# A state-space scan on one Trainium2 core: where ScalarE's softplus and layer-norm passes stand among the scan's own instructions

## What is computed

```python
def _L2_attn_ref(x, in_proj_w, conv_w, conv_b, x_proj_w, dt_proj_w, dt_proj_b, A_log, out_proj_w):
    # x_in, z = in_proj(x);  x_conv = silu(causal conv of x_in)
    B_ssm, C_ssm = ssm_params[..., :N], ssm_params[..., N:2 * N]       # N = 16 states
    dt = jax.nn.softplus(ssm_params[..., -1:] * dt_proj_w[None, None, :, 0] + dt_proj_b)
    dA = jnp.exp(dt[..., None] * A[None, None])
    dBx = dt[..., None] * B_ssm[:, :, None, :] * x_conv[..., None]
    # for every t:  h = dA_t * h + dBx_t;  y_t = sum over n of h[n] * C_t[n]
    y = y * jax.nn.silu(z)
    return jnp.einsum('btd,ed->bte', y, out_proj_w)

x = x + _L2_attn_ref(_layernorm(x, axis=-1), ...)
x = x + _L2_ffn_ref(_layernorm(x, axis=-1), ...)
```

## Time and profile before

| | |
|---|---|
| median of three runs | 1135.53 us (1133.86 to 1138.03) |
| the profiled execution | 1137.95 us |
| its span in the profile | 1136.1 us |
| mean granted TensorE clock | 0.956 of full speed |
| TensorE / VectorE / ScalarE / GpSimd busy | 1007.3 / 625.2 / 533.7 / 195.4 us |

### The profile page before, as it was taken

The page is one execution under the profiler, slowest core; times in us unless marked ns, Lnnn a source line. Parts: engine busy times, 40 slices in busy tenths (PEclk is TensorE's granted clock), DMA queues, the critical chain, the costliest instruction groups (busy, mean ns, idle before and its releaser), DMA issues.

```text
span 1136.1 us, 11530 instructions
## 1 busy us (share of the span) xinstructions
PE 1007.3 (89%) x3667; PEld 439.0 (39%) x3694; DVE 625.2 (55%) x1163; ACT 533.7 (47%) x978; POOL 195.4 (17%) x173
## 2 busy tenths in 40 slices
PE   5799999999799999998877996868788999999896
PEld 3345555454222222332233663322223444444343
DVE  2222323332888868767234445479998454545573
ACT  3232223232267667666732442665665424564540
POOL 9100000000000000000274551245663000000000
PEclk9799999999899999999988997979999999999998
DMA  8620000030011211210012426000000311110032
GB/s 176 210 84 1 1 1 1 1 91 0 22 50 43 71 43 44 60 31 1 8 33 53 128 83 189 8 4 1 0 1 1 94 49 48 48 42 19 1 111 74
DMA packets 67021, 54.70 MB, mean 48 GB/s; under 512 B 18584, under 2 KB 58830, under 8 KB 66869
## 3 DMA queue, kind: packets, MB, share of 16 engines
q1 hardware_dynamic: 64660, 51.26, 16.2%
q0 software_dynamic: 2304, 2.76, 0.8%
HBM read 41.65 MB, written 13.77 MB: 49 GB/s over the span
## 4 chain that ended last, share of the span: by engine, by line
PE 67%; DVE 13%; issue 8%; ACT 7%; DMA 2%; POOL 2%; SPq 1%; another core or an unknown queue 0%; DVEq 0%; POOLq 0%; ACTq 0%
PE psum L689 64%; ACT sb_scr L1651 4%; DVE sb_scr L2335 3%; DVE sb_scr L2683 2%; DVE sb_scr L2692 2%; ACT psum L1651 1%; ACT sb_qstack L1651 1%; POOL sb_scr L672 1%; PE psum L846 1%; PE psum L1262 1%; PE psum L1244 1%; DVE sb_scr L2210 0%; DVE sb_x L2186 0%; POOL expert_in L650 0%; DMA sb_scr<-pick_rows 0%
## 5 line engine op out<-in xcount | busy, mean ns | idle before, releaser
L1651 ACT ACTIVATE sb_scr<-psum 128x512 f32<-128x512 f32 (+3 forms) x640 | 318.5, 536 | 367.6 <-PE psum L689 291.1
L689 PE MATMUL psum<-sb_h,sb_wide 128*128 128x512 f32 x448 | 211.5, 601 | 0.8 <-ACT sb_scr L1651 0.8
L2335 DVE TENSOR_REDUCE sb_scr<-psum 128x2 f32<-128x1024 f32 x128 | 154.8, 1222 | 47.2 <-PE psum L689 46.6
L689 PE MATMUL psum<-sb_scr,sb_wide 128*128 128x512 f32 x256 | 126.2, 594 | 0.8 <-DVE sb_scr L2738 0.8
L689 PEld LDWEIGHTS psum<-sb_h,sb_wide 128*128 128x128 f32 x448 | 83.8, 193 | 93.9 <-issue 92.2
L689 PE MATMUL psum<-sb_kstack,sb_qstack 96*128 96x512 bf16 x256 | 98.8, 397 | 11.2 <-DVE sb_scr L2335 8.3
L2274 DVE TENSOR_SCALAR sb_scr<-psum,sb_b 128x512 f32<-128x512 f32 x48 | 34.5, 747 | 127.3 <-PE psum L689 127.3
L672 POOL TENSOR_TENSOR sb_scr<-sb_scr 128x512 f32<-128x512 f32 x64 | 82.9, 1300 | 98.2 <-ACT sb_scr L1651 52.0
L1651 ACT ACTIVATE sb_scr<-psum,sb_b 128x512 f32<-128x512 f32 x48 | 31.3, 685 | 138.3 <-PE psum L689 138.3
L689 PE MATMUL psum<-sb_qstack,sb_kstack 128*128 128x512 bf16 x233 | 90.5, 394 | 4.4 <-ACT sb_scr L1651 3.2
L643 POOL COPY sb_wide<-sb_wide 128x512 f32<-128x512 f32 x4 | 2.5, 623 | 513.1 <-ACT sb_scr L1651 513.1
(11 more groups left out here) (272 smaller groups left out, 1297.4 us busy)
## 6 DMA issues: line engine op xcount, KB each, us to landing
sb_scr<-weight_rows SPq DMA_DIRECT2D x32, 256.0 KB
sb_qstack<-q_bounce SPq DMA_DIRECT2D x48, 96.0 KB
sb_kstack<-k_bounce SPq DMA_DIRECT2D x144, 32.0 KB
sb_scr<-pick_rows SPq DMA_DIRECT2D x8, 512.0 KB
expert_in<-sb_scr SPq DMA_DIRECT2D x4, 645.0 KB, 6.6
sb_scr<-expert_in SPq DMA_DIRECT2D x8, 322.5 KB
expert_out<-sb_scr SPq DMA_DIRECT2D x4, 512.0 KB, 5.0
sb_scr<-expert_out SPq DMA_DIRECT2D x8, 256.0 KB, 4.7
```

Of the source, the lines that this page charges most:

```text
L689: return nc.tensor.matmul(out_, w, r, start=start, stop=stop, **kw)
L1651: return nc.scalar.activation(out_, in_, func, **kw)
L2335: v.reduce_max(headmax[:, g % 2, t:t + 2, j], banks, AX.X).then_inc(sem("maxed"), 1)
```

## The change

The three passes of a softplus no longer stand in one bunch (batch 1 behind `take_b` of state 2, batch 2 of state 5, batch 3 of state 8), but one behind the `take_b` of each of states 2 to 10. Copy and Square of a norm, both in iteration 8 before, are in iterations 7 and 8 now; Ln and Exp, both in iteration 11, are in 10 and 11. All of these norm passes stand between the decay and the `take_b` of their iteration, as before. The passes behind the scan (batch 3's norm) and the softplus of batch 0 keep their places. TensorE, VectorE, GpSimd and SyncE keep their lists.

```diff
--- before.py
+++ after.py
@@ -1911,15 +1911,17 @@
                 act.wait_ge(sem("ln_logged"), n)
                 f(rstd[:, b, :], rstd[:, b, :], ACT.Exp, scale=-0.5).then_inc(sem("ln_rstd"), 1)
 
-            def softplus(b):
-
-                n = 3 * b
-                act.wait_ge(sem("dtv_ready"), b + 2 if b else 1)
-                f(dtl[:, b, :], dtv[:, b, :], ACT.Abs).then_inc(sem("dtl_step"), 1)
-                act.wait_ge(sem("dtl_step"), n + 1)
-                f(dtl[:, b, :], dtl[:, b, :], ACT.Exp, scale=-1.0).then_inc(sem("dtl_step"), 1)
-                act.wait_ge(sem("dtl_step"), n + 2)
-                f(dtl[:, b, :], dtl[:, b, :], ACT.Ln, bias=one[:]).then_inc(sem("dtl_step"), 1)
+            def softplus_step(b, k):
+
+                if k == 0:
+                    act.wait_ge(sem("dtv_ready"), b + 2 if b else 1)
+                    f(dtl[:, b, :], dtv[:, b, :], ACT.Abs).then_inc(sem("dtl_step"), 1)
+                if k == 1:
+                    act.wait_ge(sem("dtl_step"), 3 * b + 1)
+                    f(dtl[:, b, :], dtl[:, b, :], ACT.Exp, scale=-1.0).then_inc(sem("dtl_step"), 1)
+                if k == 2:
+                    act.wait_ge(sem("dtl_step"), 3 * b + 2)
+                    f(dtl[:, b, :], dtl[:, b, :], ACT.Ln, bias=one[:]).then_inc(sem("dtl_step"), 1)
 
             for b in range(NB):
                 square(NB * ATTN2, b, 2)
@@ -1936,23 +1938,26 @@
                     take_step_size(0)
                     f(bc_raw, psum[0:2 * NSTATE, 7, :], ACT.Copy).then_inc(sem("dtv_ready"), 1)
             nc.scalar.preload_act_table_set(LOG_EXP)
-            softplus(0)
+            for k in range(3):
+                softplus_step(0, k)
             take_step_size(1)
 
             NSCAN = NB * NSTATE
             COPIES_AHEAD = 3
 
-            def copy_and_square2(b):
-                act.wait_ge(sem("ln_centered"), NB * FFN2 + b + 1)
-                f(centered3, bank(OUT_BANKS[b]), ACT.Copy)
-                f(squares3, bank(OUT_BANKS[b]), ACT.Square).then_inc(sem("ln_squared"), 1)
-
-            def deviation2_next(b):
+            def norm_step2(b, k):
                 n = NB * FFN2 + b + 1
-                act.wait_ge(sem("ln_var"), n)
-                f(rstd3, bank(OUT_BANKS[b]), ACT.Ln, bias=eps[:]).then_inc(sem("ln_logged"), 1)
-                act.wait_ge(sem("ln_logged"), n)
-                f(rstd3, rstd3, ACT.Exp, scale=-0.5).then_inc(sem("ln_rstd"), 1)
+                if k == 0:
+                    act.wait_ge(sem("ln_centered"), n)
+                    f(centered3, bank(OUT_BANKS[b]), ACT.Copy)
+                if k == 1:
+                    f(squares3, bank(OUT_BANKS[b]), ACT.Square).then_inc(sem("ln_squared"), 1)
+                if k == 2:
+                    act.wait_ge(sem("ln_var"), n)
+                    f(rstd3, bank(OUT_BANKS[b]), ACT.Ln, bias=eps[:]).then_inc(sem("ln_logged"), 1)
+                if k == 3:
+                    act.wait_ge(sem("ln_logged"), n)
+                    f(rstd3, rstd3, ACT.Exp, scale=-0.5).then_inc(sem("ln_rstd"), 1)
 
             def take_b(i):
                 act.wait_ge(sem("b_done"), i + 1)
@@ -1979,14 +1984,12 @@
             for i in range(NSCAN):
                 if i >= 1:
                     decay_of(i)
-                if i >= NSTATE and i % NSTATE == 8:
-                    copy_and_square2(i // NSTATE - 1)
-                if i >= NSTATE and i % NSTATE == 11:
-                    deviation2_next(i // NSTATE - 1)
+                if i >= NSTATE and i % NSTATE in (7, 8, 10, 11):
+                    norm_step2(i // NSTATE - 1, (7, 8, 10, 11).index(i % NSTATE))
                 if i + COPIES_AHEAD < NSCAN:
                     take_b(i + COPIES_AHEAD)
-                if i in (2, 5, 8):
-                    softplus(i // 3 + 1)
+                if 2 <= i < 3 * NB - 1:
+                    softplus_step((i - 2) // 3 + 1, (i - 2) % 3)
 
             SILU_TANH, SQRT = "silu_and_others", "sqrt_and_others"
 
@@ -2081,10 +2084,12 @@
             act.wait_ge(setup, SETUP.index("half_b") + 1)
             nc.scalar.preload_act_table_set(SILU_TANH)
             silu2(0)
-            copy_and_square2(NB - 1)
+            norm_step2(NB - 1, 0)
+            norm_step2(NB - 1, 1)
             silu2(1)
             nc.scalar.preload_act_table_set(LOG_EXP)
-            deviation2_next(NB - 1)
+            norm_step2(NB - 1, 2)
+            norm_step2(NB - 1, 3)
             act.wait_ge(sem("attn3_loaded"), 16 * 9)
             f(a_par[:, 1:2], a_par[:, 0:1], ACT.Abs).then_inc(sem("act_setup"), 1)
             act.wait_ge(sem("act_setup"), 5)
```

## The result

| | before | with the change |
|---|---|---|
| median of 19 runs each | 1136.76 us (1132.41 to 1146.11) | 1142.0 us (1135.7 to 1151.82) |
| ratio | | 1.0043, 95% interval 1.0022 to 1.0064 |
| the profiled execution | 1137.95 us | 1140.11 us |
| its span | 1136.1 us | 1138.3 us |
| mean granted TensorE clock | 0.956 | 0.955 |

The change costs 4.9 us (2.5 to 7.3 by the interval).

What follows compares the result with a forecast made beforehand. VectorE was the engine to watch in the 64-state scan, its waits there ending with ScalarE's decay. Softplus -1.4 plus norm passes +8.9 gave +7.5 us: 1143.0 from the 1135.53 median, range 1138.5 to 1146.0.

Steps and rivals of the forecast that it cites:

- the caught-up rival: Whole kernel: only 5.7 us of the norms' loss stays, with the whole 2.5 softplus gain; +3.2, 1138.7 us; chance 0.24.
- the 0.5% that the forecast claimed to pass: Whole kernel: a slowdown just past 0.5% (5.7 us), what a measurement tells from no change; slower by more: 0.66.
- Norm passes: Scan batches 1 to 3: early Copy and Ln wait for TensorE and hold ScalarE's queue; +2.96 us each, +8.9 in all.
- 1.36 - 0.40 + 0.25 + 1.26: VectorE, per batch: delay at state 24, wait swallowed at 25, new wait before 26, delay at 27, in us.
- Line 2705: normalize2_next on VectorE comes later, meets a GpSimd product already running, and ends about 0.5 later: +0.49 us a batch.
- The lower bound of 1.9 a batch: Norm passes: five waits of 0.2 us behind the place take up part of the loss; 5.7 us over three batches.
- Softplus, -1.4: First batch, states 2 to 10: single passes overlap better than bunches, so state 16 comes 1.4 us earlier.
- the 3 us that the prediction named as a sign of error: First batch: shorter by over 3 us would show the prediction wrong; state 16 about 1.4 earlier would show it right.
- The collision that the prediction saw for batch 3's multiplication: First batch, line 2656: comes to lie under a GpSimd product, taking 1.7 us for 0.69; 1.1 lost again.
- bounds of -2.5 and -0.5: Softplus at state 16: -2.5 us if the collision stays away, -0.5 if half of the overlap does not come.
- Clock rival: Batches 1 to 3: longer TensorE gaps bring a slow stretch in each, 3.9 us added; +11.4, 1146.9 us; chance 0.07.
- Faster: Whole kernel: passes fit ScalarE's waits before the copies, Copy and Ln start at once; -6.3 us, 1129.2; chance 0.07.

Runs made afterwards that it cites:

- filler: spare 512-column TensorE matmuls into an unused PSUM bank in the first batch, added to four kernels to hold the granted clock up; ratios 1.001, 0.9991, 0.9985, 1.0132.
- norms_moved_only: the change's norm steps (Copy, Square, Ln, Exp in iterations 7, 8, 10, 11) with softplus in its old bunches; ratio 1.0108 to the kernel before.
- busy_after: the change itself plus spare TensorE matmuls in the first batch; ratio 1.0132 to the kernel before, from four of its five runs.
- matmuls_first: the change, with centring and variance matmuls at the head of TensorE's iterations 5 and 8, ahead of the spreads; ratio 1.0061 to the kernel before.
- softplus_spread_only: softplus one pass a state as in the change, norm passes in their old iterations 8, 8, 11, 11; ratio 0.999 to the kernel before.
- busy_spread: softplus one pass a state behind the copy, norms as before, plus spare TensorE matmuls in the first batch; ratio 0.9991 to the kernel before.
- ln_early: kernel before with only the Ln early (Copy, Square, Ln, Exp in iterations 8, 8, 10, 11), softplus in bunches; ratio 1.0047.
- copy_early: kernel before with only the Copy early (Copy, Square, Ln, Exp in iterations 7, 8, 11, 11), softplus in bunches; ratio 1.0053.
- norms_split_late: kernel before with Copy in iteration 8, Square in 9, Ln and Exp in 11, softplus in bunches; ratio 0.9998.
- softplus_before_copy: kernel before with softplus one pass a state, between the decay and `take_b`, norms as before; ratio 1.0015.
- busy_before: the kernel before plus spare TensorE matmuls in the first batch (10 ahead, 2 behind each of states 0 to 14); ratio 1.001.

## Why the prediction was right, and where not

Forecast 1143.0 (+7.5), measured 1142.0 and +4.9 (2.5 to 7.3). The sign, the mechanism and the place were right. In size the measurement lies between the forecast and the caught-up rival (+3.2), and at 0.43% it is under the 0.5% that the forecast claimed to pass. The median comes nearer than the difference does because the kernel before had 1136.76 here, 1.2 above the median that the forecast started from.

**Norm passes, 2.96 a batch: 2.83.** This term held in each of its parts. Waits of Copy and Ln: about 1.5 forecast, 1.39. Before states 24 and 27: 1.4 and 1.5 forecast, 1.25 and 1.34. Idle time of VectorE: 1.36 - 0.40 + 0.25 + 1.26 = 2.47 forecast, 2.33. Line 2705: +0.49 forecast, 0.50 more VectorE work in the batch, 1.17 for 0.68. The lower bound of 1.9 a batch (five waits of 0.2 take some of it up) and with it the mechanism of the caught-up rival fell: nothing took anything up, and the two early passes add up, 0.92 and 1.91. Three batches at 2.83 are 8.5 us.

**Softplus, -1.4: the step whose working failed.** In the pair of profiles state 16 came 3.3 earlier, over the 3 us that the prediction named as a sign of error. The first sign was right (state 3 forecast 1.3 earlier, 1.42). At state 6 it was 3.29 for 2.2. The hand calculation had kept TensorE's slow stretches where the trace of before had them, but they moved: in the change's profile the first one, about 10 us long before, was over after some 3. Windows of the change's profile show it: PEclk is 0.50 up to 738 and 1.00 from 739 on, while before had 0.50 from 742 to 744, 8.6 to 10.6 us after its state 0:

```profile
736.00:738.00 2.00, 2.00 (x5) 0.68 (x4) 1.04 (x2) 1.48 (x3) 0.81 (x1) 0.50 0.20 49
...
739.00:742.00 3.00, 2.33 (x7) 0.53 (x5) 2.28 (x4) 2.94 (x6) 1.84 (x2) 1.00 0.00 0
742.00:744.00 2.00, 1.36 (x4) 0.50 (x4) 2.00 (x3) 1.26 (x3) 0.74 (x2) 1.00 0.00 0
```

A later slow stretch, from 756 to 769, fell where VectorE seldom waits; it cost about 1.2 before states 15 and 16 (0.63 and 0.75, for 0.20 before). The other half was luck with GpSimd. The collision that the prediction saw for batch 3's multiplication did come (1.64 for 0.69), but three that stood in the trace of before went away, so the six step sizes took 6.00 instead of 7.86; 1.86 of the 3.29 us are that. With filler the same edit gives -2.7 at state 6, and at state 16 +0.4 to +0.6 as measured, about -0.7 without the wait that goes with a slow stretch. So -1.4 with bounds of -2.5 and -0.5 was a false precision: a single profile's first batch wanders by 2.6 us (40.16 to 42.77) without any edit in it. For the whole kernel the runs say -1.1 us (-3.6 to +1.4), which holds the -1.4 but does not bear it out.

**Sum.** 8.5 less some 1.1 is +7.4; the runs say +4.9 (2.5 to 7.3). norms_moved_only came out at +12.3 (7.2 to 17.5), above its 8.5 and from six runs: the median of the six is 8.9 above that of the kernel before, and 6.4 without the two longest. The two ratios meet the sum only at the edges of their intervals. Part of what lies between goes with the clock, below; the rest stays open, and so does how much of the nearness of 1142.0 to 1143.0 is luck.

**Clock rival.** Its condition, a slow stretch in each of the batches, did not come in batches 1 and 3, with TensorE's longest gap in batch 1 at 1.5 us for the 1.8 forecast. One did come in batch 2 (PEclk 0.95 from 805.38 to 841.10, that batch 35.72 for 34.91), so the three batches were 9.3 us longer in this profile and not 8.5. All four kernels with Copy and Ln both early had one near the end of batch 2, at 0.7 to 0.9 us: the change, norms_moved_only (35.78), busy_after and matmuls_first. Of the nine others two had one at its start (softplus_spread_only, 33.79 for 32.10, and busy_spread). So it comes without the early passes too; whether they make it likelier was not tried. **Faster** fell with the first row: Copy and Ln do not start at once.

## What to carry to other kernels

In an in-order queue a pass is cheap only behind its input: before moving one earlier, find what produces its input on the other engine and what stands right behind the pass; here the producer stood behind the very spread that the next instruction was waiting for, and a wait of 0.53 us became one of 1.39. Splitting a bunch shortens the first waits, but the gain counts only at the end of the stage, where collisions with another engine and later waits may have taken it back. Where one stretch varies by 2.6 us between profiles of the same code, as the first batch here, read an effect from stretches that repeat, and leave the rest to many runs.

## What the runs showed of the hardware that was not expected

**The clock's slow stretches wander, and the noise goes with them.** Over 80 runs of the kernel before (83 less the three longest), a mean granted clock lower by 0.01 goes with 8.0 us more (correlation -0.81). Reading each kernel's runs at a clock of 0.956 by its own such line gives, as an estimate, 1137.2 before, 1143.5 with the change, 1143.6 for norms_moved_only (less its two longest), 1143.1 for ln_early, 1139.1 for copy_early (less its longest; 1141.3 with it), 1138.4 for matmuls_first, 1136.9 for softplus_spread_only, 1137.5 for norms_split_late and 1134.9 for softplus_before_copy. That is nearly the order in which the batches stand, norms_moved_only is no longer apart from the change, and the change costs 6.3 us. The kernels with filler, whose clock the filler raised, cannot be read so.

**At the end of the scan a slow stretch costs 5 to 7 us.** From the scan of state 63 to the last gate there are 5.2 us in the profile of before, and 10 to 12 in those of softplus_spread_only, busy_spread, matmuls_first and copy_early. Windows of the kernel before and of matmuls_first:

```profile
872.00:876.00 4.00, 3.28 (x14) 1.65 (x12) 1.38 (x3) 0.00 (x0) 0.00 (x0) 1.00 0.00 0
876.00:880.00 4.00, 3.94 (x9) 1.82 (x10) 3.59 (x39) 0.80 (x2) 0.00 (x0) 1.00 0.01 2
```

```profile
872.00:876.00 4.00, 4.00 (x16) 2.97 (x14) 0.85 (x2) 0.00 (x0) 0.00 (x0) 0.50 0.00 0
876.00:880.00 4.00, 4.00 (x9) 1.94 (x8) 0.21 (x1) 0.00 (x0) 0.00 (x0) 0.50 0.00 0
880.00:884.00 4.00, 3.22 (x4) 1.18 (x4) 2.06 (x14) 0.00 (x0) 0.00 (x0) 0.50 0.00 0
```

TensorE is the bound there, and at 0.50 (1.2 GHz) its matmuls take longer (a pair of spreads 1.01 for 0.60); VectorE's last read and the gate waited 3.15 and 4.37 us for it, where they wait 0.84 and 1.86 in the kernel before:

```profile
875.52 0.69 DVE L2697 TENSOR_TENSOR sb_scr<-psum,sb_scr 128x512 f32<-128x512 f32 x1 [3.15 <-PE psum L689]
880.59 0.69 DVE L2702 TENSOR_TENSOR sb_ygate<-psum,sb_scr 128x512 f32<-128x512 f32 x1 [4.37 <-PE psum L689]
```

So matmuls_first, 1.7 us a batch better than the change, gave 6.7 back at its tail in the profiled run (11.87 for 5.20), and seven of its twelve runs lay at a mean clock of 0.949 or less. Whether its order brings this or it was chance was not tried.

**Filler raises the clock.** With it the first batch's granted clock was 0.96 (busy_before; 0.92 in busy_spread and busy_after) instead of 0.80, and state 16 stood at 40.67 for 42.77, at no measurable change in the kernel's time (1.001). One of the five executions of busy_after took 4165.38 us at a mean granted clock of 0.23; the other four took 1145.88 to 1153.32. It was not followed up.
